# Wq fetched in float32 through the staging ring, between gb and Wo, and cast by ACT: an adaLN block on eight cores

## The reference, cut to what matters

```
mod = silu(c) @ wmod                      # six rows of 1024: sa, ca, ga, sb, cb, gb
ga, gb = sign(.) * max(|.|, 0.25)
h = layernorm(x) * (1 + ca) + sa          # x: 2048 x 1024 on each core
q = relu(h Wq^T) / 8;  k = relu(h Wk^T) / 8;  v = h Wv^T;  u = silu(h Wu^T)
kv = k^T v   (per head, 16 heads of 64, over all 2048 tokens)
out = srms_norm(q kv) * u
x = x + ga * (out Wo^T)
h = layernorm(x) * (1 + cb) + sb
x = x + gb * (int8-like quantized h @ quantized weight^T * scales + bias)
```

## Time and profile before

| | |
|---|---|
| median of three runs | 458.42 us (458.16 to 458.90) |
| the profiled execution | 458.85 us, its span on core 4 457.3 us |
| spans, cores 0 to 7 | 455.8, 450.7, 455.2, 451.7, 457.3, 451.4, 456.1, 451.2 us |
| busy on core 4 | PE 390.0, DVE 273.9, ACT 235.6, POOL 96.9 us |
| DMA on core 4 | 87.05 MB, 190 GB/s on average |
| chain that ended last | PE 45%, DMA 17%, DVE 13%, issue 8%, ACT 7%, SP's queue 6%, POOL 3% |

### The profile page before, as it was taken

The page is one execution under the profiler, slowest core; times in us unless marked ns, Lnnn a source line. Parts: engine busy times, 40 slices in busy tenths (PEclk is TensorE's granted clock), DMA queues, the critical chain, the costliest instruction groups (busy, mean ns, idle before and its releaser), DMA issues.

```text
span 457.3 us, 6430 instructions; the slowest of 8 cores (450.7 to 457.3 us)
## 1 busy us (share of the span) xinstructions
PE 390.0 (85%) x2022; PEld 185.4 (41%) x2062; DVE 273.9 (60%) x487; ACT 235.6 (52%) x342; POOL 96.9 (21%) x148
## 2 busy tenths in 40 slices
PE   3043799849998999988898899999999999999983
PEld 1020444425544545434443344444444443444432
DVE  4557902175692644467845875568565755766885
ACT  3342553527257433768656854476825577443532
POOL 2514701040064011000011202121212131202421
PEclk9995699979999999998999999999999999999999
DMA  7999699949985999999698615634564574265796
GB/s 194 280 262 335 159 171 245 330 131 299 339 303 185 195 311 292 216 245 352 200 365 273 130 46 96 137 84 101 93 120 93 110 139 85 64 128 94 125 149 140
DMA packets 20914, 87.05 MB, mean 190 GB/s; under 512 B 2825, under 2 KB 3089, under 8 KB 17042
## 3 DMA queue, kind: packets, MB, share of 16 engines
q0 software_dynamic: 8544, 31.49, 37.9%
q1 hardware_dynamic: 12338, 55.16, 36.0%
HBM read 70.36 MB, written 24.67 MB: 208 GB/s over the span
## 4 chain that ended last, share of the span: by engine, by line
PE 45%; DMA 17%; DVE 13%; issue 8%; ACT 7%; SPq 6%; POOL 3%; DVEq 0%; ACTq 0%; POOLq 0%
PE pb L368 32%; PE pb L842 8%; DMA xr<-x_tm 8%; SPq L44 6%; DMA wa<-wmod_a 5%; DMA stage<-wmod_b 5%; DVE stage L436 3%; ACT rn L704 2%; DVE h L790 2%; DVE am L793 2%; DVE wm_c L492 2%; PE pb L702 1%; DVE bn L302 1%; ACT rn L707 1%; PE pb L819 1%
## 5 line engine op out<-in xcount | busy, mean ns | idle before, releaser
L368 PE MATMUL pb<-h,wu_s 128*128 128x512 bf16 x251 | 61.5, 386 | 1.6 <-ACT u_s L681 1.2
L368 PE MATMUL pb<-wo_s,u_s 128*128 128x512 bf16 x251 | 59.4, 379 | 1.2 <-DVE u_s L684 1.0
L842 PE MATMUL pb<-fq,xqT 128*128 128x512 bf16 (+1 forms) x255 | 58.7, 372 | 1.7 <-ACT xqT L824 1.3
L368 PE MATMUL pb<-wv_s,h 128*128 128x512 bf16 x249 | 59.2, 387 | 0.9 <-ACT kT L384 0.4
L368 PE MATMUL pb<-h,wq_s 128*128 128x512 bf16 x249 | 59.6, 379 | 0.4
L436 DVE SCALAR_TENSOR_TENSOR stage<-stage,silr 128x1024 f32<-128x1024 f32 x32 | 37.7, 1219 | 20.8 <-DMA stage<-wmod_b 20.8
L368 PE MATMUL pb<-wk_s,h 128*128 128x512 bf16 x203 | 45.4, 379 | 0.6 <-DMA wk_s<-wk 0.3
L709 DVE SCALAR_TENSOR_TENSOR q_s<-rn,pb 128x512 bf16<-128x512 f32 x32 | 22.0, 686 | 29.7 <-ACT rn L707 29.3
L302 DVE BATCH_NORM_STATS2 bn<-xr 128x6 f32<-128x512 f32 x26 | 16.7, 684 | 37.0 <-DMA xr<-x_tm 37.0
L368 PEld LDWEIGHTS pb<-h,wu_s 128*128 128x128 bf16 x256 | 24.9, 99 | 31.1 <-issue 4.5
L368 PEld LDWEIGHTS pb<-wo_s,u_s 128*128 128x128 bf16 x256 | 24.9, 98 | 31.0 <-issue 1.4
(11 more groups left out here) (104 smaller groups left out, 577.2 us busy)
## 6 DMA issues: line engine op xcount, KB each, us to landing
stage<-wmod_b SPq DMA_DIRECT2D x16, 1024.0 KB, 11.6
xr<-x_tm SPq DMA_DIRECT2D x21, 512.0 KB, 4.6
wa<-wmod_a SPq DMA_DIRECT2D x16, 512.0 KB, 20.7
out_tm<-row_gbb SPq DMA_DIRECT2D x4, 2048.0 KB, 17.4
out_tm<-xr POOLq DMA_DIRECT2D x15, 512.0 KB, 7.9
out_tm<-h POOLq DMA_DIRECT2D x15, 512.0 KB, 5.3
xr<-x_tm POOLq DMA_DIRECT2D x8, 512.0 KB, 19.8
stage<-wo SPq DMA_DIRECT2D x4, 1024.0 KB, 6.2
```

The lines of the kernel that those rows point to most:

```text
L368: t = PE.do(lambda e, dc=dc: e.matmul(pb[bank][:], lhs(dc), rhs(dc), start=(dc == 0), stop=(dc == NC - 1)), *after, each(dc) if each else ...
L842: t = PE.do(lambda e, ic=ic, sl=sl, ps=ps: e.matmul(ps, xqT[a][:, ic], fq[:, ic, sl], start=(ic == 0), stop=(ic == NC - 1)), free, xqT_tok ...
```

## The change

Wq leaves POOL's casting DMAs. It becomes four float32 pieces of the staging ring, numbers 16 to 19, and ACT casts each into `wq` with two copies. The order of the ring is now ga, sb, cb, gb, Wq, Wo, ffn: 28 pieces for 24. The first stage load waits for both halves of `wv` (before, for the first). Groups x10 and x11 are read ahead of the second half of `wv`. The jobs stand at other places of the loops: three in `vproj(0)`, four in `vproj(1)`, eight in `kproj(2)`, the last of gb at `vproj(2)`'s start, the four casts in the second half of `kproj(3)`, Wo in `vproj(3)`.

```diff
-    stream = ([(d_wb, (v * NC + 2 * c) * D, 4 * NC * D) for v in range(3) for c in range(4)]
+    stream = ([(d_wb, (v * NC + 2 * c) * D, 4 * NC * D) for v in range(4) for c in range(4)]
+              + [(d_w["wq"], 2048 * k, NC * D) for k in range(4)]
               + [(d_wo, 2 * c * D, NC * D) for c in range(4)]
-              + [(d_wb, (3 * NC + 2 * c) * D, 4 * NC * D) for c in range(4)]
               + [(d_fw, 2 * c * D, NC * D) for c in range(4)])
...
+    def cast_piece(w, dst, k):
+
+        n = AT[w] + k
+        s = stage[n % SR]
+        hf, c = divmod(4 * k, NC)
+        for d in range(2):
+            w_tok[w, hf] = ACT.do(lambda e, d=d: e.copy(
+                out=dst[:, hf, c + 2 * d:c + 2 * d + 2],
+                in_=s[:, D * d:D * d + D].rearrange("p (c e) -> p c e", c=2)), st_tok[n], wa_free[NC - 1])
+        staged(n, w_tok[w, hf])
...
     load_w("wv", wv, 0)
-    for g in (8, 9):
+    for g in range(8, 12):
         more_x(g)
     load_w("wv", wv, 1)
-    for g in (10, 11, 12):
-        more_x(g)
+    more_x(12)
     for n in range(SR):
-        load_stage(n, w_tok["wv", 0])
+        load_stage(n, w_tok["wv", 1])
...
-    mods[12:12] = [lambda c=c: wo_piece(c) for c in range(4)]
+    mods += [lambda k=k: cast_piece("wq", wq, k) for k in range(4)]
+    mods += [lambda c=c: wo_piece(c) for c in range(4)]
...
-        mod()
         if n >= 5:
+            mod()
             kvprod(0, n - 5)
...
-    load_w("wq", wq, 0, wa_free[NC - 1])
-    row(1, row_sb)
-    load_w("wq", wq, 1)
-    row(2, row_cb)
-    for h in range(2):
-        load_w("wu", wu, h)
     for n, (hf, j) in enumerate(eight):
         kproj(2, hf, j)
...
+        mod()
+        if n == 0:
+            row(1, row_sb)
+        if n == 4:
+            row(2, row_cb)
+            for h in range(2):
+                load_w("wu", wu, h)
...
     for n, (hf, j) in enumerate(eight):
         kproj(3, hf, j)
+        if n > 3:
+            mod()
...
     for n, (hf, j) in enumerate(eight):
         vproj(3, hf, j)
+        mod()
+        if n == 3:
+            get(3, row_g, fold_tok[0])
```

More of the change, by code:

```diff
@@ L242, in build_nc @@
     wa_free = {}
-    stream = ([(d_wb, (v * NC + 2 * c) * D, 4 * NC * D) for v in range(3) for c in range(4)]
+    stream = ([(d_wb, (v * NC + 2 * c) * D, 4 * NC * D) for v in range(4) for c in range(4)]
+              + [(d_w["wq"], 2048 * k, NC * D) for k in range(4)]
               + [(d_wo, 2 * c * D, NC * D) for c in range(4)]
-              + [(d_wb, (3 * NC + 2 * c) * D, 4 * NC * D) for c in range(4)]
               + [(d_fw, 2 * c * D, NC * D) for c in range(4)])
-    AT = {"ga": 0, "sb": 4, "cb": 8, "wo": 12, "gb": 16, "ffn": 20}
+    AT = {"ga": 0, "sb": 4, "cb": 8, "gb": 12, "wq": 16, "wo": 20, "ffn": 24}
     def load_stage(n, *after):
@@ L610, in build_nc @@
             stats(12 + n)
-        if n == 3:
+        else:
+            mod()
+        if n == 4:
             row(0, row_g)
-        mod()
-    load_w("wq", wq, 0, wa_free[NC - 1])
-    row(1, row_sb)
-    load_w("wq", wq, 1)
-    row(2, row_cb)
-    for h in range(2):
-        load_w("wu", wu, h)
     for n, (hf, j) in enumerate(eight):
@@ L624, in build_nc @@
             kvprod(1, 3)
-        if n < 4:
-            mod()
-        else:
+        if n > 3:
             xhat(8 + n)
-    row(3, row_g, fold_tok[0])
-    put(4, gbb_c, col_tok[3])
-    get(4, row_gbb)
+        mod()
+        if n == 0:
+            row(1, row_sb)
+        if n == 4:
+            row(2, row_cb)
+            for h in range(2):
+                load_w("wu", wu, h)
     for n, (hf, j) in enumerate(eight):
         vproj(2, hf, j)
+        if n == 0:
+            mod()
+            put(3, mod_c[3], col_tok[3])
+            put(4, gbb_c, col_tok[3])
+            get(4, row_gbb)
         if n >= 5:
```

## The result

The changed kernel takes 470.74 us (median of four runs, 469.80 to 471.08), the kernel before 458.66 beside it (458.16 to 459.96): a ratio of 1.0256, interval 1.0229 to 1.0282, 12 us slower. The forecast was 463.9, with a range of 453 to 469. Now and then an execution of any of these kernels takes 26 to 42 us more, with a lower clock on one die; ratios and spreads leave these out, and the medians of experiments 2, 4 (the second) and 9 hold one each.

What follows compares the result with a forecast made beforehand. First pass taken as bound by PE, a few microseconds from DMA-bound. Gaps of 11.0 us go, but late Wq pieces put the second pass at 189.8, 5.5 later: 458.85 + 5.5 = 464.3, median 463.9; range 453 to 469.

Steps and rivals of the forecast that it cites:

- What the change removes: First pass, PE's gaps at 92 to 101 us and at 141.9: they go, 11.0 us in sum.
- What ACT pays: Last four kproj(3) calls: two casts of 1.24 us each per call; the casts alone cost PE 2.7 us.
- `wu`'s transfer: Before the second pass: `wu` starts moving at 151 us behind `row_cb`, takes two thirds of the DMAs, is over at 170.
- The rival in which they keep two thirds: Stage loads keep two thirds of the DMAs against `wu`: second pass at 186.3, time 460.4; chance 0.13.
- row_cb takes 5 us: `row_cb`, issued at 146 us with `wu` behind it, takes 5 us, so `wu` starts moving at 151.
- check by bytes: Whatever the shares, `wu` and the four Wq pieces are 8.4 MB, some 26 us, and end at 177 at the latest.
- one busy queue: From piece 6 (about 117 us) on, the DMAs are never idle; piece 15 is in at 149.5.
- Start of the second pass: Last cast ends at 178.0, and 11.2 us after the first vT bank empties the second pass starts: 189.8, 5.5 later.
- recovers in the calls that run between the three waits: PE's clock falls to 1.2 GHz in the waits but recovers, nothing added; if not, 1.73 us more.
- Four cores may lose more, but hardly pass it: Cores 1, 3, 5, 7, with spans some 5 us shorter, may lose more, but hardly pass the others' time.
- Any wait here is swallowed by the larger one below.: PE's wait for `wv`'s second half at the fifth vproj call, 0 to 0.5 us, taken as none.
- Feeding on itself: Last five vproj(3) calls at 1.2 GHz, 8.7 us more, and Wo pieces hold DVE past q evictions: 472; chance 0.09.

Runs made afterwards that it cites:

- experiments 2: Changed kernel with only the second half of `wu` held until the last Wq piece is cast: 469.75 us, ratio 1.0217.
- 4 (the second): Changed kernel with the casts of Wq on DVE in place of ACT and the folds of Wo moved into the second pass: 456.30 us, ratio 0.9941.
- experiment 9: Kernel before, with first stage loads waiting for `wv`'s second half and statistics of x12 to x15 four places earlier on DVE: 448.77 us, ratio 0.9775.
- experiment 8: Kernel before with x10 and x11 ahead of `wv`'s second half: 454.50 us; also stage loads waiting for that half: 456.04; that wait alone: 453.58.
- experiment 6: Changed kernel with the first stage loads waiting for the first half of `wv`, as before the change: 471.46 us, ratio 1.0262.
- experiment 7: Changed kernel with x10 and x11 behind `wv`'s second half again and stage loads from the first half on: 479.01 us, ratio 1.0439.
- experiments 1: Changed kernel with both loads of `wu` issued only after the last Wq piece is cast: 469.73 us, ratio 1.0223.
- experiment 4: Changed kernel with the casts of Wq on DVE in place of ACT, at the same places: 467.10 us, ratio 1.0175.

## Why the prediction was wrong in size and right in sign

- **What the change removes.** Right: no gap at 92, the statistics of the last of x8 to x11 at 77.65 us, 10.5 us won on core 0 for 11.0 predicted on core 4. It gave the credit to the x order and the wait together; experiment 8 shows that the wait alone closes the gap.
- **What ACT pays.** The pair of casts took 1.99 us where 2.48 was taken from the normalization. That error was in the kernel's favour.
- **`wu`'s transfer.** Right to 0.2 us: counted from `row_cb`'s landing, 148.3 + 11.9 = 160.2, to 179.4 it is 19.2 us; 19 were predicted. The share of the stage pieces beside it, one third of the time, also held: 33.3% between 160 and 176 us, and 9.4 and 9.5 us from piece to piece. The rival in which they keep two thirds is refuted.
- **The term that was mis-sized: `row_cb`.** "row_cb takes 5 us" is the step that failed. It took 11.9 (6.4 to 13.0 on the eight cores), and it was issued at 148.3, not 146. The row that was nearest said 7.6, and the text went below it without a bound above, though the same trace has 6.9 to 11.3 for this load on its eight cores.
- **How this reaches the last piece.** Not by the later start of `wu` alone. That gave pieces 16 and 17 more of the DMAs (their casts start at 157.31 and 166.75, for 160 and 169 predicted), and by the forecast's own check by bytes the last piece comes when the bytes ahead of it are through, in whatever order. But the sum had `row_cb` over at 151, before pieces 16 to 19, and its check counted `wu` and the four pieces alone. Its half MB was moved among them. The two queues of core 4 between 151 and 179 us:

```profile
q0 software_dynamic: 496, 2.63, 54.4%
q1 hardware_dynamic: 563, 4.09, 45.6%
```

POOL's queue moves 2.63 MB, the 2.10 of `wu` and 0.52 of `row_cb`, in 54.4% of 28 us = 15.2 us of the engines, 2.5 more than two thirds of 19; the pieces take the 12.8 that the sum gave them. So from piece 15 to piece 19 it is 28.3 us on this core (DVE takes up piece 15 at 150.57, ACT piece 19 at 178.91) and 29.1 on core 0 (151.97 and 181.02), for 26.0 predicted. Piece 15 itself was 1.1 and 2.5 us later than the 149.5 of the sum; the text took "one busy queue" from piece 6 on, and the DMA share between 117 and 150 us was 0.96 on core 4 and 0.92 on core 0, which is 1.3 and 2.6 us of idle DMAs. No run took `row_cb` away, so this share of the miss is read from the trace and not tested.
- **Start of the second pass.** On core 4, of which the sum was made, 192.79 us for 189.8 predicted, 3.0 of the miss, from the last piece: 3.4 later than predicted, and its pair of casts 0.5 shorter (the last cast ended at 180.9 for 178.0). Its span was 9.0 us over before's, for 5.5. The slowest core became core 0, with a span another 3.0 us longer: its last cast was 2.1 later, and from there to the second pass it took 1.4 more (0.5 came back behind it), since three more calls began at the low clock where the text said "recovers in the calls that run between the three waits". It didn't on this core: three calls of 3.33 to 3.57 us, and the clock at 0.50 in 180 to 185. The text had a price of 1.73 for this, and left it out of the sum. 463.9 + 3.5 + 3.0 = 470.4, of 470.74.
- **The other cores.** "Four cores may lose more, but hardly pass it": of these, core 3 passed core 4 in the profiled run (468.2 for 466.3; its second pass starts at 193.68, 15.1 us later than before), and cores 1 and 5 were the slowest of all in another. The late core of a pair changes from run to run, and the time of the kernel is that of the latest of eight, so a sum made on one core should have been read as a middle, not as the slowest.
- **"Any wait here is swallowed by the larger one below."** The forecast lost nothing by it: PE has no wait for `wv` in the changed kernel, and in experiment 6 one of 3.84 us costs nothing. As a rule it would be false: in experiment 7 an early wait is not swallowed, since the late groups that make it also put back `wu` and Wq.
- **Feeding on itself.** DVE folded Wo by 198.4 us (191 predicted), still ahead of the first q eviction at 201.79, so that wait didn't appear. It was 3 us away, and experiments 1 and 4 made it the bound. This rival's number, 472, is the nearest to the measured one, and that is luck: of its 8.7 us at the low clock in the last five calls 1.5 came, and the wait for DVE not at all.

The forecast named the chain (transfer, ACT in order, PE) and what would show it; what it lacked was a bound for `row_cb` above the one row it had, its bytes in the check, and a reading of the other cores.

## What to carry to other kernels

Before a job that waits for a transfer is put on an engine that also empties PSUM banks, ask what the transfer is worth at its worst, since every bank behind it pays: here 8 us of casts on ACT, in four pairs, came with 17 us of waits on PE. Moving the load that is in the way helps only if nobody else waits in order beside its new place; here moving the waiter helped more than moving the load (1.0175 against 1.0223 by itself, 0.9941 against 1.0050 with Wo folded late). And where a gap comes from contention, hold back the transfer that isn't wanted yet: one token (the second half of `wv` for the first) gave 1.2%, and with the statistics moved 2.2%.

## What was not expected of the hardware

- A row read back and spread over 128 partitions (0.5 MB written) took 6.4 to 13.0 us from issue to landing on the eight cores, with stage pieces in flight beside it, and 6.9 to 11.3 in the kernel before (POOL's queue moved nothing at all between 148 and 152 us on core 0, though the load was issued at 148.32); on core 0 of the changed kernel the rows ga and sb took 10.7 and 9.1. Whether it is its own pattern or its share beside the pieces that makes it slow was not separated, and stays open. The Trainium skill, page "DMA: Bandwidth & Descriptors", section "Queues, rings and completion order", has each engine take turns between its queues, whole packets at a time. The trace agrees: beside `wu` the two queues moved 238 and 235 packets in 16 us. It gives no time for a packet: by 68.7% and 33.3% of 16 engines' time, those of the casting load took about twice as long, and a piece took 9.4 to 9.5 us beside `wu` against 3 to 5 without it.
- A put and its get without a casting load ahead in POOL's queue took some 7 us from issue to issue (141.26 to 148.32), against the 18.71 us wait of before. Two later puts stood behind `wu` in that queue (the last issued at 156.82), and POOL waited 24.31 us for them.
- A copy of 128x1024 from float32 to bf16 in SBUF took ACT 1.04 us (changed kernel) and DVE 0.65 (a pair of 1.29, experiment 4), for the 1.24 of ACT's normalization of the same shape.
- Neighbouring cores part by up to 12 us in the changed kernel, whose DMA share is 1.01 between 155 and 190 us, and a different one of the two is late in different runs. In the profiled run of the kernel before the spans of two neighbours differed by 3.5 to 6 us (up to 8 in others), and in that of experiment 9 by 2.2 to 4.5. That the two share a limit is only argued; no run took one of them away.
